# Fifteen batch loops written as loops of the machine instead of being unrolled

## The reference

```python
x = x + attn_a(_layernorm(x), Wk, Wv, Wo, gate, freqs)
x = x + ffn(_layernorm(x), cn_w1..cn_b4, gc_w1..gc_b3, adaptive_range)
x = x + attn_b(_layernorm(x), z_q, b_q, z_k, b_k, w_v, b_v)
x = x + ffn(_layernorm(x), cn_w1..cn_b4, gc_w1..gc_b3, adaptive_range)
```

## Time and profile before

| | us |
|---|---|
| median of three runs | 3053.67 |
| lowest, highest | 3051.18, 3056.8 |
| the profiled execution | 3053.67 |
| its span, first to last instruction | 3051.9 |

### The profile page before, as it was taken

The page is one execution under the profiler, slowest core; times in us unless marked ns, Lnnn a source line. Parts: engine busy times, 40 slices in busy tenths (PEclk is TensorE's granted clock), DMA queues, the critical chain, the costliest instruction groups (busy, mean ns, idle before and its releaser), DMA issues. The chain is left out here.

```text
span 3051.9 us, 52239 instructions
## 1 busy us (share of the span) xinstructions
PE 2726.2 (89%) x20897; PEld 1245.4 (41%) x20897; DVE 1872.7 (61%) x2420; ACT 2019.9 (66%) x2650; POOL 1281.2 (42%) x786
## 2 busy tenths in 40 slices
PE   2799999999997999953999999999999999789997
PEld 1355555555554444321333333333333433244443
DVE  8899999999994445356455554555555441144444
ACT  6454454555433555531989999989999999745564
POOL 3788998998892122035323232323232220022110
PEclk7899999999998999976999999999999999989999
DMA  2010010001003121123454554545454546232112
GB/s 83 1 35 21 28 42 28 28 28 35 14 21 104 42 69 56 56 82 63 76 96 101 90 106 85 112 77 119 76 120 73 109 73 121 58 90 69 42 41 69
DMA packets 164083, 201.60 MB, mean 66 GB/s; under 512 B 16505, under 2 KB 118273, under 8 KB 163841
## 3 DMA queue, kind: packets, MB, share of 16 engines
q1 hardware_dynamic: 163840, 198.25, 28.6%
HBM read 139.49 MB, written 58.72 MB: 65 GB/s over the span
## 5 line engine op out<-in xcount | busy, mean ns | idle before, releaser
L1870 ACT ACTIVATE b_pr<-b_ps 128x1024 f32<-128x1024 f32 x1024 | 999.8, 1035 | 142.6 <-PE b_ps L1889 136.5
L1889 PE MATMUL b_ps<-b_st 128*32 128x512 bf16 x8192 | 621.1, 381 | 34.2 <-ACT b_pr L1870 26.3
L1955 PE MATMUL b_acc<-b_pr,b_vaug 128*32 128x512 f32 x4096 | 535.7, 592 | 3.5 <-DVE b_osb L1758 3.2
L1889 PEld LDWEIGHTS b_ps<-b_st 128*32 128x32 bf16 x8192 | 185.9, 95 | 580.4 <-ACT b_pr L1870 354.8
L1257 PE MATMUL f_po<-f_s,f_w 128*128 128x512 f32 x768 | 354.8, 605 | 9.5 <-DVE f_xr L1042 5.6
L1030 DVE TENSOR_TENSOR f_turned<-f_cs,f_s 128x1024 f32<-128x1024 f32 x96 | 119.0, 1239 | 364.9 <-ACT f_cs L1159 359.5
L635 PE MATMUL a_pv<-a_xnT,a_wv 128*128 128x512 f32 x512 | 250.9, 614 | 55.9 <-DVE a_mem L403 41.8
L1123 ACT ACTIVATE f_h<-f_po,f_b 128x512 f32<-128x512 f32 x192 | 131.9, 687 | 216.8 <-PE f_po L1257 216.8
L627 PE MATMUL a_pu<-a_xnT,a_wk 128*128 128x512 f32 x512 | 235.3, 603 | 30.8 <-DVE a_frac L355 25.4
L1586 POOL TENSOR_TENSOR b_SQ<-b_A 128x1024 f32<-128x1024 f32 x32 | 66.6, 2083 | 455.6 <-DVE b_A L1683 455.6
L674 PE MATMUL a_py<-a_wo,a_out 128*128 128x256 f32 x960 | 231.9, 385 | 0.0
(11 more groups left out here) (261 smaller groups left out, 4558.7 us busy)
## 6 DMA issues: line engine op xcount, KB each, us to landing
b_st<-b_scratch SPq DMA_DIRECT2D x512, 128.0 KB, 7.0
b_scratch<-b_parts SPq DMA_DIRECT2D x32, 768.0 KB, 5.1
f_xl<-x SPq DMA_DIRECT2D x16, 1024.0 KB, 5.5
f_xr<-x SPq DMA_DIRECT2D x16, 1024.0 KB, 7.3
a_xl<-in_L_attn_a_x_dram SPq DMA_DIRECT2D x16, 512.0 KB, 4.4
x<-a_xr SPq DMA_DIRECT2D x32, 256.0 KB, 2.1
x<-f_xr SPq DMA_DIRECT2D x8, 1024.0 KB, 4.4
b_xl<-x SPq DMA_DIRECT2D x8, 1024.0 KB, 8.3
```

Of the source, the lines that this page charges most:

```text
L1870: nc.scalar.activation(pr[:, 4 * (blk % 2) + j, :], ps[:, j % 2, :], ACT.Exp, scale=SC).then_inc(S["probs_done"], 1)
L1889: x = nc.tensor.matmul(o[r:r + 32], w[:, r:r + 32], v, start=start, stop=stop, skip_group_check=True)
L1955: x = nc.tensor.matmul(acc[32 * j:32 * j + 32, h * 512:(h + 1) * 512], vaug[:, kt, c:c + 32], pr[:, 4 * (kt % 2) + j, h * 512:(h + 1) * 51 ...
```

## The change

Each of fifteen Python loops over the batches (or pairs) becomes a loop of the engine that runs it: `engine.Fori(a, b)` writes its body once, keeps the index in a register of that engine, and ends with an addition and a compare-and-branch back to the body's beginning. The ranges stay the same. The same edit stands at L225 (SP), L337 (POOL), L460 (DVE), L596 (ACT), L712 (PE) in phase_a; L960, L1003, L1089, L1177, L1315 in phase_f; L1538, L1622, L1818, L1875, L2005 in phase_b. No engine waits for the others at the branch. B is 8 and PAIRS is 4.

```diff
@@ phase_a, SP @@
-                for b in range(0, B - 2):
+                with sp.Fori(0, B - 2) as b:
                     load_xl(b + 2)
                     batch(b)
@@ phase_a, DVE (POOL, ACT and PE alike) @@
-                for b in range(1, B - 1):
+                with dve.Fori(1, B - 1) as b:
                     batch(b)
@@ phase_f, PE (SP, POOL, DVE and ACT alike) @@
-                for j in range(1, PAIRS - 1):
+                with pe.Fori(1, PAIRS - 1) as j:
                     pair(j)
@@ phase_b, ACT (SP, POOL, DVE and PE alike) @@
-                for b in range(1, B - 2):
+                with act.Fori(1, B - 2) as b:
                     batch(b)
```

More of the change, by code:

```diff
@@ L336, in _ @@
                 batch(0, first=True)
-                for b in range(1, B - 1):
+                with pool.Fori(1, B - 1) as b:
                     batch(b)
@@ L595, in _ @@
                 batch(0, first=True)
-                for b in range(1, B - 1):
+                with act.Fori(1, B - 1) as b:
                     batch(b)
@@ L711, in _ @@
                 batch(0, first=True)
-                for b in range(1, B - 1):
+                with pe.Fori(1, B - 1) as b:
                     batch(b)
@@ L959, in _ @@
                 pair(0, first=True)
-                for j in range(1, PAIRS - 1):
+                with sp.Fori(1, PAIRS - 1) as j:
                     pair(j)
@@ L1002, in _ @@
                 pair(0, first=True)
-                for j in range(1, PAIRS - 1):
+                with pool.Fori(1, PAIRS - 1) as j:
                     pair(j)
@@ L1088, in _ @@
                 pair(0, first=True)
-                for j in range(1, PAIRS - 1):
+                with dve.Fori(1, PAIRS - 1) as j:
                     pair(j)
@@ L1176, in _ @@
                 pair(0, first=True)
-                for j in range(1, PAIRS - 1):
+                with act.Fori(1, PAIRS - 1) as j:
                     pair(j)
@@ L1537, in _ @@
                 batch(0, first=True)
-                for b in range(1, B - 2):
+                with sp.Fori(1, B - 2) as b:
                     batch(b)
@@ L1621, in _ @@
                 batch(0, first=True)
-                for b in range(1, B - 2):
+                with pool.Fori(1, B - 2) as b:
                     batch(b)
@@ L1817, in _ @@
                 batch(0, first=True)
-                for b in range(1, B - 2):
+                with dve.Fori(1, B - 2) as b:
                     batch(b)
@@ L2004, in _ @@
                 batch(0, first=True)
-                for b in range(1, B - 2):
+                with pe.Fori(1, B - 2) as b:
                     batch(b)
```

## The result

| | median us | lowest, highest | runs |
|---|---|---|---|
| before, measured beside it | 3052.43 | 3047.14, 3056.80 | 4 |
| after | 3090.32 | 3087.33, 3092.50 | 4 |

The ratio is 1.0125, with a 95% interval of 1.0105 to 1.0143: 37.9 us more. The forecast was 3097 us in a range of 3057 to 3148. The sum was 7 us off, but most of its terms were not as forecast, and that is what the rest is about.

What follows compares the result with a forecast made beforehand. Bound by stage: DVE in phase_a, PE in phase_f, PE and ACT waiting on each other in phase_b. 3053.7 us plus jumps 24, moved waits 14 and 5, gave 3097 us, range 3057 to 3148.

Steps and rivals of the forecast that it cites:

- Jumps in phase_a and phase_f, 10 + 4 us: Refetch after each jump partly uncovered: 5 x 2.0 us in phase_a, 2 x 2.0 us in phase_f.
- The third rival: Short bodies stay on chip in phase_a and phase_f; only phase_b's PE body is fetched again; 3082 us, chance 0.18.
- Jumps in phase_b, 9.6 us: At phase_b's four jumps PE's refetch stays open 2.4 us each; ACT's own fetch nearly covered and beside PE's.
- The price of 3.4 us for a fetch: Any jump back: 2.2 us for a small load to land plus 1.25 us for one 16 KB packet.
- the upper bound, 8.2 us: Fetch after a jump if its request takes as long as phase_b's 128 KB loads: 7.0 + 1.25 us.
- The cover on PE: At phase_b's jump, already queued score matmuls and a weighing hide about 1.0 us of the 3.4 us fetch.
- Register arithmetic, 0: Added register instructions on all engines hide in queues ahead; without cover, 55 us on PE in phase_b.
- Moved waits in phase_a, 0: Most changed waits in phase_a are POOL's and on PE's output projection, which DVE does not wait for: 0.
- Moved waits, 14 + 5 us: Sequencer waits delay phase_b's first exponential of each block by 0.15 us, 14 us; late waits in phase_f, 5 us.
- In series: Rival: two engines' fetches do not overlap, 75 us, and exposed register work is 30 us; 3159 us, chance 0.15.

Runs made afterwards that it cites:

- e12: Kernel after, but one pass of phase_a's POOL, DVE, ACT and PE loops does three batches; 3098.41 us, ratio 1.0141.
- e6: Kernel after with SP's phase_b transfers (second half of the parts, b_xl load) moved away from the jump; 3070.49 us, ratio 1.0050.
- e4: Only ACT's batches of phase_b are a loop, all else written out as in the kernel before; 3076.00 us, ratio 1.0087.
- e8: Kernel after with a hint at the top of each pass of PE's and ACT's phase_b loops announcing the jump back; 3075.74 us, ratio 1.0067.
- e14: Kernel before, no loops, with the gathers of groups 2 and 3 waiting for 12 more tiles of scores; 3068.03 us, ratio 1.0055.
- e9: Kernel after with PE's and ACT's phase_b batches written out again, the other thirteen loops kept; 3054.52 us, ratio 1.0010.
- e3: Kernel before with only PE's batches of phase_b made a loop; 3084.59 us, ratio 1.0107.
- e11: As e4, but ACT's loop in phase_b begins at the start of a fetch block; 3076.56 us, ratio 1.0087.

## Why the prediction was right and where it was not

The kernel got slower by 38 us where 43 were forecast, for the reason named first, the fetch behind the jump. By its steps:

- **Jumps in phase_a and phase_f, 10 + 4 us: wrong, 0.** A taken branch of PE lasts 0.21 to 0.23 us there, and DVE's step across the jump 12.74 us like any other. The step that failed is that a body's beginning is fetched again at every jump. The third rival had it right: PE's 680 and 642 recorded instructions, DVE's 187 and ACT's 146 and 191 stay on the chip. Its word on ACT in phase_b was not: with 418 instructions ACT does fetch, 4.3 to 6.8 us, while DVE's 278 do not. e12 makes the same bodies three times as long, and PE, DVE and ACT fetch.
- **Jumps in phase_b, 9.6 us: right in kind, less than half its size.** On the exponentials the four jumps cost 3.4, 5.9, 6.3 and 6.0 us, in all 21.6. The price of 3.4 us for a fetch was that of a quiet moment: 3.5 to 3.8 us in e6. I had not asked what else is on its way at the jump; the upper bound, 8.2 us, had the right idea, a fetch that lands like a bulk load. The cover on PE was 1.8 us instead of 1.0: 4.57 us of branch left 2.75 us open, 7.02 us left 5.21. ACT's fetch was not nearly covered: alone, in e4, it costs 3.4 to 5.8 us at a jump.
- **Missing from the sum:** the clock behind the jump, 2.4 + 1.2 + 2.1 = 5.7 us; and stalls in straight code, 1.0 us at the end of batch 0, 3.9 in batch 4, 1.1 in batch 5 and 1.6 at the end of batch 6, where before had 0.9 us in batch 3 and 1.3 in batch 4, so 5.4 us more. The longest looks like those of e8 and e14: PE stands 2.02 us for `issue` in front of the matmul at 2153.11, and a packet of q8 landed 1.38 us before it. That says late fetches; for the kernel after itself no experiment shows it.
- **Register arithmetic, 0: near.** e9 has it on three engines in phase_b and on five elsewhere, and phase_b does not grow.
- **Moved waits in phase_a, 0: a small miss, 2.6 us.** Of the 0.43 us of each looped batch, 0.28 stand where DVE waits for PE once a batch (L408 for a_pv of L635) and 0.15 where it waits for ACT (L355 for L523). The pass with no jump behind it has them too, so they belong to register work or moved waits, which no run here separates. So DVE does wait for PE and ACT once a batch, and a batch is not eight steps of 12.73 us.
- **Moved waits, 14 + 5 us: wrong, about 1.** Apart from the stalls named, the five looped batches of phase_b grew by 1.0 us together. ACT's waits for scores grew only from 185 to 191; that the sequencer does this work while the exponential before is running would explain it, and was not tried apart. A pair of phase_f, which lasts 87.5 us and not the 93 that I read from the stretch, changed by 0.05 us.
- **In series:** e3 and e4 cost 32.8 and 24.2 us alone; the changed kernel costs 37.9 with both. The fetches run beside each other.

Phase_b adds up: 21.6 + 5.7 + 5.4 + 1.0 = 33.7 us, where its span grew by 33.8. That the whole sum came so near is luck: errors of opposite sign met. Too much was put on phase_a (10 us for 2.6), on phase_f (9 us for nearly nothing) and on phase_b's moved waits (14 us for 1), 29 us in all; 12 us too little on phase_b's jumps; and 11 us of clock and straight-code stalls were not thought of: 43 - 29 + 12 + 11 = 37, beside the 37.9 us of the medians. The profiled executions differ by less, 34.7, mostly as phase_a had two more of its short batches after, 3.4 us.

The Trainium skill (Runtime: NRT & Kernel Launch, section "Instruction fetch mechanics") says that a branch out of the engine's window waits for a fetch. The branches of 4.6 to 7.4 us agree. Its sizes of 512 instructions, and 2048 on PE, agree with DVE's 187, 278 and 557 and PE's 680, but not with ACT's 418 and 416 or PE's 2028, all counted as recorded, which would have fitted and were fetched again (ACT's 418 also with its head at a block's start, in e11). It also calls the fetch of a straight stream mostly hidden: here that holds until bulk transfers fill the queues, as the 5.70 us of e14 show.

## What to carry to other kernels

Before making a batch a loop on the chip, count the instructions of the body for each engine and look at which of them are without slack: short bodies were nearly free here (thirteen of fifteen loops together: ratio 1.0010), two long ones on the engines that set the time cost 38 us. Price the fetch by what the DMA queues carry at that moment, 3.6 us when quiet and 7 us behind 2.5 MB, not by its own size. And read `<- issue` on PE in straight code in the same way: a bulk load issued just ahead of the next fetch stops the engine with nothing in the profile to wait for.

## What the runs showed of the hardware

- The program's own packets wait behind the data's: a fetch began 0.9 to 1.5 us after the branch where SP's transfers were moved away (share 0.01 at the jump shown), 4.6 to 4.9 us after it with the share at 1.0, and PE's branch ended 1.2 to 1.6 us after it had landed.
- Idle stretches of 5.2 to 5.7 us on PE (three jumps, and the 88th exponential of e14) were each followed by 3.4 to 4.0 us at a granted clock of 0.50 to 0.53. Shorter ones go either way: behind 2.75 us and 1.78 us the clock was 1.00, behind the 2.00 us of e6's second jump 0.68 over 3.9 us, where the exponentials lost 1.7 us.
- The hint for the jump back took the branch from 7 us to 0.4 to 1.2 us, while SP's transfers stood where they did.
